# A graph network kernel: tile tables built between the first pass's groups, a buffer for every product chunk, x's rows loaded in 13 transfers

## The reference

```python
def _L0_gnn_ref(z, edge_weight, edge_src, edge_dst, Wm, bm, W1, b1, W2, b2):
    Wd, Ws, ww = (Wm[:H], Wm[H:2 * H], Wm[2 * H])
    msgs = z[edge_dst] @ Wd + z[edge_src] @ Ws + edge_weight[:, None] * ww[None, :] + bm
    agg = jax.ops.segment_max(msgs, edge_dst, num_segments=n)
    deg = jax.ops.segment_sum(jnp.ones_like(edge_weight), edge_dst, num_segments=n)
    agg = jnp.where(deg[:, None] > 0, agg, jnp.zeros((), dtype=z.dtype))
    hidden = jax.nn.relu(z @ W1a + agg @ W1b + b1)
    return hidden @ W2 + b2
x = _layernorm(x + _L0_gnn_ref(x, ...), axis=-1)
x = _layernorm(x + _L1_gnn_ref(x, ...), axis=-1)
```

## Time and profile before

| | us |
|---|---|
| median of 3 runs | 2215.26 (2212.79 to 2216.94) |
| the profiled execution's own time | 2217.47 |
| its span | 2215.7 |
| POOL busy | 1612.1 (73%), 1703 instructions |
| PE busy | 1641.7 (74%) |
| DVE busy | 1319.9 (60%) |
| ACT busy | 1128.0 (51%) |

### The profile page before, as it was taken

How to read it: one execution, slowest core, us unless ns; L and a number is a source line. 1 busy time by engine, 2 the same in 40 slices (tenths; PEclk the granted TensorE clock), 3 DMA queues, 4 the chain that set the end, 5 groups by cost and what they waited for, 6 DMA issues and landing times. The chain is left out here.

```text
span 2215.7 us, 43419 instructions
## 1 busy us (share of the span) xinstructions
PE 1641.7 (74%) x9963; PEld 1000.0 (45%) x9963; DVE 1319.9 (60%) x5221; ACT 1128.0 (51%) x3319; POOL 1612.1 (73%) x1703
## 2 busy tenths in 40 slices
PE   5877777787788888944877677766777676777774
PEld 5222222222233323213646566655666565665664
DVE  4765566556554554444766666666666666665669
ACT  3434343333444444621666666555656566655548
POOL 5767777777777777777677777777777777777635
PEclk8989999999899999975989989899888999889888
DMA  8453444343434434435522222222222222222213
GB/s 277 160 184 128 130 130 130 128 150 115 145 130 136 133 122 149 151 110 113 181 67 66 66 66 66 62 65 66 61 66 65 66 60 66 66 62 65 62 57 119
DMA packets 115985, 235.06 MB, mean 106 GB/s; under 512 B 32910, under 2 KB 68231, under 8 KB 106423
## 3 DMA queue, kind: packets, MB, share of 16 engines
q0 software_dynamic: 52832, 109.39, 20.4%
q1 hardware_dynamic: 56522, 97.21, 12.0%
q10 hardware_dynamic: 6540, 27.42, 3.5%
HBM read 166.01 MB, written 67.89 MB: 106 GB/s over the span
## 5 line engine op out<-in xcount | busy, mean ns | idle before, releaser
L461 POOL DMA_INDIRECT d_region<-d_h,d_region x784 | 755.8, 964 | 248.0 <-issue 209.5
L214 POOL DMA_INDIRECT acc<-d_src_product,b_region x760 | 718.4, 945 | 251.8 <-issue 200.6
L907 DVE SCALAR_TENSOR_TENSOR banks<-banks,b_region,acc 128x128 f32<-128x128 f32 x784 | 277.1, 354 | 419.2 <-DMA acc<-d_src_product,b_region 418.6
L1683 DVE TENSOR_TENSOR acc<-acc,banks 128x160 f32 x784 | 252.3, 322 | 220.4 <-PE banks L1482 84.4
L689 PE MATMUL banks<-acc,b_region 64*128 64x512 f32 x1176 | 318.9, 649 | 35.9 <-ACT acc L795 18.4
L1448 PE MATMUL banks<-shift_ident,d_region 128*128 128x128 f32 x784 | 135.1, 297 | 249.6 <-DMA d_region<-d_h,d_region 237.9
L917 DVE SCALAR_TENSOR_TENSOR acc<-acc,b_region,banks 128x128 f32<-128x128 f32 x784 | 264.3, 337 | 0.0
L1479 PE MATMUL banks<-d_region 128*128 128x128 f32 x1568 | 247.9, 310 | 0.2 <-DVE d_region L1644 0.2
L1482 PE MATMUL banks<-d_region,pick 128*128 128x128 f32 x1568 | 241.4, 303 | 0.0
L1479 PEld LDWEIGHTS banks<-d_region 128*128 128x128 f32 x1568 | 233.4, 227 | 1.3 <-issue 0.4
L795 ACT ACTIVATE gate_col<-banks,b_region 128x1024 f32<-128x1024 f32 x147 | 158.5, 1111 | 142.0 <-PE banks L689 140.9
(11 more groups left out here) (271 smaller groups left out, 2428.3 us busy)
## 6 DMA issues: line engine op xcount, KB each, us to landing
d_runs<-acc SPq DMA_DIRECT2D x48, 1024.0 KB, 4.4
acc<-ea ACTq DMA_DIRECT2D x25, 1024.0 KB, 5.2
d_region<-d_h,d_region POOLq DMA_INDIRECT x784
d_region<-d_rel SPq DMA_DIRECT2D x49, 256.0 KB
acc<-d_src_product,b_region POOLq DMA_INDIRECT x760
hT<-xT SPq DMA_DIRECT2D x7, 448.0 KB, 7.4
d_src_product<-acc SPq DMA_DIRECT2D x7, 448.0 KB, 7.1
d_gates<-acc ACTq DMA_DIRECT2D x196, 6.0 KB
```

The source lines that it names most:

```text
L214: pool.indirect_dma_start(self.rows[:, s, j, :], None, table, bass.IndirectOffsetOnAxis(self.idx[:, k:k + 1], 0)).then_inc(self.gathered[s ...
L461: pool.indirect_dma_start(rows[:, s, :], None, table, bass.IndirectOffsetOnAxis(idx[:, s:s + 1], 0)).then_inc(gathered[q], 16)
L907: nc.vector.scalar_tensor_tensor(stepped[:, k % STEPS, :], wwp, wgt[:, k:k + 1], rows[:, s, j, :], ALU.mult, ALU.add).then_inc(ch, 1)
L1683: nc.vector.tensor_tensor(w, w, UZ[q % 2][:, :, j, :], ALU.add).then_inc(ad, 1)
```

## The change

- Each of the 7 product chunks has its own buffer, so ACT no longer waits for a store. The buffers lie over `rec`, `dI` and the other table inputs, which are therefore loaded only when all chunks are stored.
- SP's order in the head: edges, feature weights, all 7 chunk stores, a wait until they have landed, and then the three table loads and the other weights. The out weights (att, rel, o1, o2, wout) move from `gate_col` to the end of the first two planes of `acc`.
- `tables_chain` is cut into six pieces that `extra(g)` calls after groups 3 to 7 (CHAIN_AT = 3) and 9 (NUMBER_AT = 9); `tile_starts` follows after group 11 and `tiles_of_jobs` after groups 12 to 19. PE makes the prefix sums at its group 8 (PREFIX_AT), `start_rows` at 10 and the out weights at 12, where ACT copies them as well. The tables' store and wout's move into SP's first pass, behind run stores 2 and 3. The results of PE's table products go to banks 1 and 2, which the owner rows use too.
- For that, marks, owner rows and counts begin 14 groups later (2, 0, 7 become 16, 14, 21), and so do the parts for the nodes (100 to 114 and so on). The distances between them are kept.
- x's rows are loaded in 13 transfers of 256 KB (the last 64 KB), one behind each of the run stores 5 to 17.
- EARLY_JOBS becomes 5. ACT's second load of edge features is issued behind its raw copies instead of ahead of them.

```diff
@@ phase_tables @@
-    bst = new_sems(*[f"a_b_stored{s}" for s in range(BB)])
-    ca = Carve(t["acc"][:, 0:2, :].rearrange("p a b -> p (a b)"))
+    bst, = new_sems("a_b_stored")
+    planes = t["acc"][:, 0:2, :].rearrange("p a b -> p (a b)")
+    cb, ca = Carve(planes), Carve(planes)
+    bo = [cb(CN) for _ in range(NCH)]
...
-        for s in range(BB):
-            pool.wait_ge(bst[s], 16 * len(range(s, NCH, BB)))
+        pool.wait_ge(bst, 16 * NCH)
...
         runs.load_edges(sp, i)
+        runs.load_feature_weights(sp, i)
+        for c in range(NCH):
+            store_product(c)
+        sp.wait_ge(bst, 16 * NCH)
         sp.dma_start(dI, tiles(i["dst"], 1)).then_inc(ld, 16)
         sp.dma_start(prevI, tiles(i["dst"], 0)).then_inc(ld, 16)
         sp.dma_start(srcI, tiles(i["src"], 0)).then_inc(ld, 16)
-        store_product(0)
-        store_product(1)
-        runs.load_feature_weights(sp, i)
-        for c in range(2, NCH):
-            store_product(c)
         runs.load_out_weights(sp, i)
         runs.load_node_weights(sp, i)
+
+    def store_tiles(sp):
         sp.wait_ge(ch, CH_REC)
...
         for c in range(NCH):
-            if c == 4:
-                pe.wait_ge(ch, CH_KM)
-                nc.tensor.matmul(bank[3][:, 0:TC], upper, km, start=True, stop=False)
...
             product(c)
+
+    def prefix_sums(pe):
+        pe.wait_ge(ch, CH_KM)
+        nc.tensor.matmul(bank[1][:, 0:TC], upper, km, start=True, stop=False)
...
             act.wait_ge(pb, c + 1)
-            if c >= BB:
-                act.wait_ge(bst[c % BB], 16 * (c // BB))
...
@@ constants @@
-MARK_AT, SEL_AT, COUNT_AT, STEP = 2, 0, 7, 2
-SHIFT_AT, HAS_AT = 100, 105
-PART_PE, PART_DVE, PART_STEP = 104, 108, 5
+MARK_AT, SEL_AT, COUNT_AT, STEP = 16, 14, 21, 2
+SHIFT_AT, HAS_AT = 114, 119
+PART_PE, PART_DVE, PART_STEP = 118, 122, 5
+CHAIN_AT, PREFIX_AT, NUMBER_AT, START_AT, ROWS_AT, OUT_WEIGHTS_AT, TILES_AT = 3, 8, 9, 10, 11, 12, 12
...
-EARLY_JOBS = 6
+EARLY_JOBS = 5
 X_AT = 5
-TILES_AT = 10
+X_LOADS = 6 + NC4
@@ phase_runs, SP @@
-            sp.wait_ge(owc, 1)
-            sp.dma_start(d["wout"], wout).then_inc(ows, 16)
...
+                if b == 2:
+                    tables.store_tiles(sp)
+                if b == 3:
+                    sp.wait_ge(owc, 1)
+                    sp.dma_start(d["wout"], wout).then_inc(ows, 16)
                 if b == X_AT:
...
-                    sp.dma_start(xb.rearrange("p b f -> p (b f)"), i["xrow"]).then_inc(xl, 16)
+                    sp.wait_ge(ows, 16)
+                if X_AT <= b < X_AT + NC4:
+                    c = b - X_AT
+                    z, n = widths(c)
+                    sp.dma_start(xb[:, 4 * c:4 * c + z, :].rearrange("p b f -> p (b f)"), i["xrow"][:, c * G4:c * G4 + n]
+                                 ).then_inc(xl, 16)
@@ phase_runs, PE @@
+                if g == PREFIX_AT:
+                    tables.prefix_sums(pe)
+                if g == START_AT:
+                    tables.start_rows(pe)
+                if g == OUT_WEIGHTS_AT:
+                    out_weights()
@@ phase_runs, ACT @@
             load(0)
+            tables.raw_copies(act)
             load(1)
-            tables.raw_copies(act)
@@ phase_runs, DVE @@
-            tables.tables_chain(dve, tc)
...
+                if g == CHAIN_AT:
+                    tables.tiles_copied(dve, tc)
+                if g == CHAIN_AT + 1:
+                    tables.sources_copied(dve, tc)
+                if g == CHAIN_AT + 2:
+                    tables.starts_marked(dve, tc)
+                if g == CHAIN_AT + 3:
+                    tables.tiles_ends(dve, tc)
+                if g == CHAIN_AT + 4:
+                    tables.windows_counted(dve, tc)
+                if g == NUMBER_AT:
+                    tables.tiles_numbered(dve, tc)
+                if g == ROWS_AT:
+                    tables.tile_starts(dve, tc)
```

More of the change, by code:

```diff
@@ L239, in phase_tables @@
     ws = ca(P)
-    bo = [ca(CN) for _ in range(BB)]
     turned = [ca(G4) for _ in range(2)]
@@ L709, in owner_rows @@
                     pe.wait_ge(cnt, b)
+                else:
+                    pe.wait_ge(owc, 1)
                 nc.tensor.matmul(bank[1][:, 0:EP // 2], oh[b % 2], dF[:, 0:EP // 2], start=True, stop=True)
@@ L803, in store @@
                                   ).then_inc(gst[u % 2], 16)
-            act.wait_ge(owp, 1)
-            nc.scalar.activation(wout, bank[3][:, :], ACT.Copy, scale=1.0 / 3.0).then_inc(owc, 1)
             relus(0)
-            act.wait_ge(ows, 16)
             for g in range(PG):
@@ L822, in _ @@
                         store(u - 1)
+                if g == OUT_WEIGHTS_AT:
+                    act.wait_ge(owp, 1)
+                    nc.scalar.activation(wout, bank[2][:, :], ACT.Copy, scale=1.0 / 3.0).then_inc(owc, 1)
                 c, off = divmod(g - PART_PE, PART_STEP)
```

80 lines of the change are left out of this document (42 added, 38 removed).

## The result

| | before | changed |
|---|---|---|
| median, same chip (us) | 2217.65 (6 runs) | 2201.41 (2194.8 to 2205.44, 6 runs) |
| ratio of the changed kernel to the one before | | 0.9927, interval 0.9907 to 0.9946 |
| the profiled execution, its span | 2217.47, 2215.7 | 2203.97, 2202.2 |

A forecast was written before the change was run, and what follows sets the result against it. POOL's 760 gathers of B were taken to bound the first pass, with two holes to remove. Terms -12.45 - 5.8 + 0.5 + 0.6 = -17.15 took the median 2215.26 to 2198.1 us, range 2194.5 to 2206.5.

The forecast's parts named there:

- Hole 1: Head: POOL idles 13.73 us before its first gather of B; new buffers and SP's order gain 12.45 us (8.95 to 13.45).
- true releaser: Head: SP's last store of B, landing at about 48.3, not the DVE step named, releases POOL's first gather of B.
- Hole 2: First pass, behind x's load of 3136 KB: POOL waits 6.09 us; splitting the load gains 5.8 us.
- The pieces of x: First pass, behind 13 run stores: added traffic of 0.8 us each, taken as 0.5 us for all.
- Marks, counts and parts 14 groups later: First pass: distances kept, PE follows DVE by five groups as before; claimed to cost nothing.
- EARLY_JOBS: End of the pass: three gathers before the fix's scatter instead of two; costs 0.6 us (0 to 1.25).
- The slack: Early pass: prefix sums at 77.4, POOL's group 16 at 86.5 with six us of room, group 10 some 9 us.
- A: Head: stores land late, B's last chunk at 44; POOL gains 5 instead of 12.45, 2205.6 us; chance 0.12.
- B: First pass: each piece of x costs its full 0.8 us, 10.4 in all, 2208.0 us; chance 0.06.
- C: First pass: hole 2 stays, caused by run store and features' load together; 2203.4 us; chance 0.04.
- D: Early pass: PE's first units take 10.0 us, prefix sums at 93, POOL loses 9.6; 2207.7 us; chance 0.04.
- E: Head: nothing gained because POOL waits for DVE's first steps, reckoned ready by 26; chance 0.02.

The follow-up runs named there:

- e12: Changed kernel with three of its seven product buffers and ACT's old waits for stores, new order kept: 2202.98 us, ratio 0.9938.
- e5: Kernel before with seven product buffers, nothing else but an added ACT wait for the stores behind its raw copies: 2217.03 us, ratio 1.0005.
- e6: Kernel before with seven product buffers and PE's prefix sums behind the last product chunk: 2214.73 us, ratio 0.9987.
- e1: Kernel before with x's rows in 13 transfers behind run stores 5 to 17, nothing else: 2211.36 us, ratio 0.9971.
- e2: Changed kernel with x's rows in one transfer of 3136 KB behind run store 5: 2206.55 us, ratio 0.9947.
- e10: Changed kernel itself, timed once more: 2201.57 us, ratio 0.9923 to the kernel before.
- e8: Changed kernel with ACT's second load of edge features ahead of the raw copies again: 2203.53 us, ratio 0.9934.
- e3: Changed kernel with the 13 transfers of x's rows issued one after the other behind run store 5: 2204.52 us, ratio 0.9938.
- e4: Changed kernel with EARLY_JOBS 6 instead of 5: 2197.69 us, ratio 0.9912 to the kernel before.
- e11: Changed kernel with EARLY_JOBS 6, same as e4, timed again: 2201.96 us, ratio 0.9917 to the kernel before.
- e7: Changed kernel with the prefix sums at PE's group 12 instead of 8, later table steps moved too: 2206.47 us, ratio 0.9938.
- e9: Kernel of e6 with feature weights loaded ahead of the table loads and DVE's tile_starts behind its group 0: 2216.27 us, ratio 0.9978 to the kernel before.

## Why the prediction was right, and where it wasn't

**Hole 1** (-12.45 taken, -14.6 measured). The arithmetic of bytes held: 313 GB/s until 24 us, 309 from there to 33.4, and B had landed by 33.46 where 32.9 had been worked out. Then 2 to 3 us were added for a tail, by the 3.3 us of the quickest store, and that term was mis-sized: 0.6 us stood there. The last raw rows came only at 37.22 (PE above), 4.1 us behind their gather, with no harm to POOL. POOL's own row of raw gathers also ended 1.2 us sooner than before, at 34.03, which moved the lower bound of 35.5; why it did wasn't tried. What the prediction credited to buffers and order together is some 12 us of order and 1 to 2.4 of buffers (e12, e5). The "true releaser" was right for the kernel before (the last store took 9.7 us; the 9.9 of the earlier trace rows is another's), but the prediction didn't see how close behind it the second gate stood, which e6 ran into.

**Hole 2** (-5.8 taken). e1 measures 5.8 in the pass and 6.2 in the median, e2 gives 5 to 7: right in size. Its path was right too, but the prediction took the load's size for the whole cause; the place in the pass matters as well (the wait of 8.12 us without a hole). What was argued against the two rules of the Trainium skill's page "DMA: Bandwidth & Descriptors" holds here. Thirteen transfers in place of one (sections Bandwidth and "Anatomy of one DMA — SWDGE (gpsimd) path") didn't cost 24 us but gained 5 to 7; that section gives its fixed 2.0 us for transfers issued by GpSimd, and these are SP's, so the 24 us were an estimate from a neighbouring case. And a load on SP's queue does hold back POOL's gathers (8.79 us in e2), so the turns taken packet by packet of "Queues, rings and completion order" don't protect them here. No run tests the page's rule on throughput itself: nobody waits for this load, and the gathers beside it are what counts.

**The pieces of x** (+0.5 taken; the worst case of the range used 1.5). In the changed kernel one hole of 1.79 us, 16 us behind the twelfth piece (354.33): DVE waits 4.89 us for gathered rows at 360.97, PE 3.05 at 365.39, POOL at 370.64, the chain of the earlier trace rows in small. That the piece alone did it isn't shown: waits of this size come without any load of x as well (8.12 us above). In e10 the like follows the first piece (133.35) with 1.25 us; e1 has none. So 0 to 1.5 us over the usual issue for all 13.

**Marks, counts and parts 14 groups later** ("Cost nothing"): not quite. The hole at 128.75 stands before any piece of x, the first of which was issued at 134.29. PE ran ahead of DVE until there, which it couldn't before, then stood 12.57 us for DVE's first count. The rows: PE's timeline, and the stretches before, in and behind that wait (the seventh number is PE's granted clock).

```profile
123.51 1.65 PE L732 MATMUL banks<-b_region 128*128 128x392 f32 x2 [12.57 <-DVE b_region L972]
```

```profile
105.00:110.90 5.90, 5.54 (x24) 1.30 (x20) 5.79 (x19) 3.24 (x3) 4.38 (x6) 0.99 0.18 48
111.00:123.40 12.40, 0.00 (x0) 0.00 (x0) 8.41 (x29) 0.57 (x1) 9.36 (x11) 0.67 0.41 137
123.50:126.40 2.90, 2.89 (x5) 1.16 (x6) 1.41 (x6) 0.00 (x0) 2.29 (x3) 0.50 0.19 51
...
126.40:130.40 4.00, 3.96 (x13) 1.47 (x12) 2.87 (x10) 1.81 (x2) 2.29 (x4) 0.68 0.14 35
```

PE came back at half its clock, and for the 4 us of the next unit at 0.68. In e8 it stood as long (14.85 us) and came back as slow, but the unit behind it already ran at 0.99, and POOL has no hole there. The same two stretches of e8, and the unit behind in e3 and e4:

```profile
125.30:128.20 2.90, 2.85 (x4) 1.18 (x4) 1.46 (x6) 0.00 (x0) 2.24 (x3) 0.50 0.22 57
128.20:132.20 4.00, 3.64 (x17) 1.23 (x18) 2.70 (x10) 2.54 (x3) 2.83 (x4) 0.99 0.18 49
...
128.40:132.40 4.00, 4.00 (x13) 1.49 (x12) 2.82 (x10) 1.66 (x2) 2.28 (x3) 0.64 0.13 34
...
125.80:129.80 4.00, 3.64 (x13) 1.29 (x12) 2.90 (x10) 2.12 (x2) 2.59 (x3) 0.83 0.20 49
```

So the hole goes with the clock of that unit, and all eight executions with this wait bear it out:

| | e3 | changed | e2 | e11 | e10 | e4 | e12 | e8 |
|---|---|---|---|---|---|---|---|---|
| granted clock, the 4 us of the unit | 0.64 | 0.68 | 0.71 | 0.77 | 0.82 | 0.83 | 0.89 | 0.99 |
| POOL's hole over the usual 0.30 (us) | 0.81 | 0.80 | 0.84 | 0.72 | 0.50 | 0.51 | 0.39 | none |

That is a comparison of executions, no test of it by itself: nothing was run that changes the clock alone. The hole at 511.86 has the same look (PE waits 3.21 us for a count, then its next matmuls are slow); it stands in the changed kernel, e4, e10, e11 and e12 and in none of e1, e2, e3, e7, e8. Why DVE is late just there wasn't tried and stays open, and so is whether this term belongs to the change.

**EARLY_JOBS** (+0.6 taken): 0.8 to 1.0, nearer the upper bound.

**The slack.** DVE's numbering started at 76.74 against 77.4 forecast (its term from 29.29 to 30.84 is 1.55, not 1.45), the first unit at 41.78 against 41.9. The room of 5.7 us is near the 6 forecast, but by errors that cancel: POOL began 2.2 us earlier than reckoned, two early gathers of its row took 1.43 and 1.63 us instead of 0.95, and DVE was ready some 0.7 us earlier. DVE's wait for the table loads until 43 to 45 didn't come: the raw rows of group 3 held it until 40.71, and by then the tables were there. POOL's group 10 was said to have 9 us; through its leash on PE's dots it had 3.

**The sum.** -14.6 - 5.8 + 1.5 (piece) + 0.8 (tie) + 1.0 (at 511) + 1.0 (EARLY_JOBS) = -16.1; the medians say -16.2, e10's -17.6. The agreement to a tenth is chance: in the profiled executions the pass is 1.8 us shorter, where these terms make 2.5. The mechanism of both holes was right, but that the total came within a microsecond of 17.15 is partly luck: the term of the head was too small by 2.2, and the others, two of which (the tie and the hole at 511) the prediction had put at nothing, were off by 3.2 in the other direction.

**The rivals.** A (stores land late): B landed at 33.4, not 44. B (each piece costs): 1.5 us in all. C (hole 2 stays): e1. D (PE's units are slow): they came every 6.1 us, as reckoned. E (POOL waits for DVE's first steps) was given 0.02, rightly for the changed kernel (28.5 against 34.34), though the first steps were done by 28.5 and not by 26, and its gate is a real one: it is what e6 and e9 ran into.

## What to carry to other kernels

An engine that starts late may stand behind more than one closed gate. The trace shows the one that opened last; list the other conditions of that instruction and when each was met, because the gain of mending the first ends at the second. Here they were 2.5 us apart, and one piece of work, the table chain in the head, held both; the new order was worth 12.2 us, while more buffers alone were worth nothing.

A large load that nobody waits for yet can be spread in pieces between other work, if somebody gathers on the same DMA engines and has little slack: here that was worth 5 to 7 us, and the same pieces asked for within 9.31 us still left a hole of 4.35.

## What the runs showed of the hardware

- Beside a single load of 3136 KB on SP's queue DVE waited 8.62 to 8.79 us for the rows of POOL's gathers (the kernel before, e5, e6, e9, e2), beside 13 loads (256 KB, the last 64) issued in 9.31 us 5.71 (e3). It is not the load of x alone that does this: where a run store and a load of edge features, together 2 MB, were asked for within 1.1 us, DVE waited 8.12 us (the kernel before).
- An issue on SP's queue can take long by itself. Of e6 SP's timeline shows one small load of weights, issued behind two stores of B, whose issue took 6.72 us, with the other weights behind it. In that stretch (20.8 to 27.5 us) the DMA engines moved 384 GB/s at a share of 1.08, and ACT had asked for two loads of 1024 KB from 19.82 on. In the kernel before, behind the same two stores but without ACT's loads, the issue took 1.65 us, and 0.47 in the changed kernel ahead of all stores:

```profile
20.78 6.72 SPq L199 DMA_DIRECT2D b_region<-ww  x1
```

  PE then waited 4.26 us for the last of these weights.
- After idling for 9.4 to 14.9 us PE came back at a granted clock of 0.50 (1.2 of its 2.4 GHz) for 2.9 us in eight executions; over the next 4 us, in which it was busy, the mean was 0.64 to 0.99, different from one execution to the next.
